# Explicit softmax weights in place of two masked sums in a graph-attention, GRU and mixture-of-experts kernel

## The reference, cut to what matters

```python
h = layernorm(x)
Wh = h @ W;  src = Wh @ a[:256];  dst = Wh @ a[256:]
e = leaky_relu(src + dst.T, 0.2)
att = softmax(where(adj > 0, e, -9e15), axis=1)
gi = (att @ Wh) @ w_ih.T + b_ih
gh = h @ w_hh.T + b_hh
r, z = sigmoid(i_r + h_r), sigmoid(i_z + h_z)
x = x + (1 - z) * tanh(i_n + r * h_n) + z * h
# then: layernorm, gate logits to 16 experts, top 2, expert FFN 256 -> 512 -> 256 with silu, weighted sum, added to x
```

## Time and profile before

| | us |
|---|---|
| median of 3 runs | 1377.35 (1371.5 to 1383.42) |
| the profiled execution, its own time | 1370.29 |
| its span, first to last instruction | 1368.6 |
| outside the span | 1.7 |

### The profile page before, as it was taken

The page is one execution under the profiler, slowest core; times in us unless marked ns, Lnnn a source line. Parts: engine busy times, 40 slices in busy tenths (PEclk is TensorE's granted clock), DMA queues, the critical chain, the costliest instruction groups (busy, mean ns, idle before and its releaser), DMA issues.

```text
span 1368.6 us, 30563 instructions
## 1 busy us (share of the span) xinstructions
PE 1267.8 (93%) x8305; PEld 1101.5 (80%) x8307; DVE 1065.1 (78%) x2513; ACT 671.5 (49%) x1281; POOL 330.8 (24%) x345
## 2 busy tenths in 40 slices
PE   4668999999999999999999999637999999999995
PEld 2447989898998989899898989536888888888884
DVE  3876688787878878787887878597888888887883
ACT  3554444344444534444444444204666666666662
POOL 1011101111111011111101110004655544555554
PEclk9988999999999999999999999857999999999998
DMA  4123334333333333333343432023343455545430
GB/s 135 55 58 48 57 56 67 54 59 67 57 62 57 69 51 60 66 58 63 56 69 50 63 64 36 27 88 94 48 112 78 94 146 126 133 97 133 93 51 8
DMA packets 61970, 98.00 MB, mean 72 GB/s; under 512 B 9856, under 2 KB 36480, under 8 KB 61920
## 3 DMA queue, kind: packets, MB, share of 16 engines
q0 software_dynamic: 33600, 52.49, 25.8%
q1 hardware_dynamic: 27536, 44.14, 10.0%
q10 hardware_dynamic: 784, 0.79, 0.2%
HBM read 213.18 MB, written 18.81 MB: 170 GB/s over the span
## 4 chain that ended last, share of the span: by engine, by line
PE 83%; DMA 6%; DVE 5%; issue 3%; ACT 1%; DVEq 1%; POOL 1%; POOLq 0%; SPq 0%; ACTq 0%
PE bank L1079 37%; PE bank L1187 13%; PE bank L1201 8%; PE bank L1101 8%; PE bank L1013 6%; DMA out<-ysc,cidx 5%; PE pT L1066 4%; PE bank L1104 4%; PE bank L1120 1%; PE bank L1039 1%; ACT V L516 1%; DVE lane_hot L934 1%; POOL rstd L428 1%; DVE slot_hot L938 1%; DMA scr<-in_L_gnn_w_ih 0%
## 5 line engine op out<-in xcount | busy, mean ns | idle before, releaser
L1079 PE MATMUL bank<-V,mask 128*128 128x258 f32 x4096 | 558.4, 289 | 1.7 <-DVE comb L767 1.0
L1079 PEld LDWEIGHTS bank<-V,mask 128*128 128x128 f32 x4096 | 511.4, 190 | 2.1 <-issue 1.1
L533 ACT ACTIVATE mask<-pT 128x512 fp32r<-128x512 bf16 x512 | 277.9, 597 | 195.4 <-PE pT L1066 195.4
L1187 PE MATMUL bank<-wup,xT 128*128 128x512 f32 x948 | 239.0, 401 | 0.9 <-DVE xT L960 0.9
L1187 PEld LDWEIGHTS bank<-wup,xT 128*128 128x128 f32 x948 | 174.1, 190 | 35.0 <-DVE xT L960 1.3
L955 DVE TENSOR_TENSOR wup<-wexp,wup 128x1024 fp32r<-128x1024 f32 x158 | 185.9, 1218 | 2.2 <-ACT wup L488 1.1
L407 POOL DMA_DIRECT2D adjb<-in_adj x128 | 69.4, 542 | 479.3 <-DVE tbuf L750 455.1
L468 POOL DMA_INDIRECT out<-ysc,cidx x79 | 138.3, 1750 | 174.6 <-DMA out<-ysc,cidx 88.8
L488 ACT ACTIVATE wup<-wexp 128x1024 fp32r x158 | 165.7, 1050 | 9.7 <-DMA wexp<-in_L_ffn_w 9.2
L745 DVE CUSTOM_DVE_ANT_0 gbuf<-Dp,adjb 128x1024 bf16<-128x1024 f32 x128 | 156.3, 1221 | 4.0 <-DVE tbuf L750 0.7
L1201 PE MATMUL bank<-wexp,hidT 128*128 x632 | 150.0, 380 | 2.0 <-DVE ysc L993 1.1
(11 more groups left out here) (148 smaller groups left out, 1327.1 us busy)
## 6 DMA issues: line engine op xcount, KB each, us to landing
wexp<-in_L_ffn_w SPq DMA_DIRECT2D x237, 512.0 KB
adjb<-in_adj POOLq DMA_DIRECT2D x128, 256.0 KB, 4.3
token_rows<-xrow SPq DMA_DIRECT2D x32, 130.0 KB, 2.5
adjb<-in_x SPq DMA_DIRECT2D x32, 128.0 KB, 2.1
xin<-in_x SPq DMA_DIRECT2D x32, 128.0 KB, 2.4
out<-xin SPq DMA_DIRECT2D x32, 128.0 KB, 3.3
xg<-token_rows,gidx POOLq DMA_INDIRECT x79, 3.5
out<-ysc,cidx POOLq DMA_INDIRECT x79, 3.8
```

Source lines behind the costliest of these rows:

```text
L533: ins = nc.scalar.activation(mask[:, c % 2, k, :], pT[c % 2][:, 0:MC], ACT.Relu, scale=sign)
L1079: ins = mm(acc[:, 0:VW], mask[:, c % 2, k, b * P:(b + 1) * P], V[:, j, 2 * k + part, :], start=j == 0 and part == 0, stop=j == T - 1 and p ...
L1187: ins = mm(acc[:, 0:HID], xT[:, r % WR, a, k * P:(k + 1) * P], wup[:, r % 2, n, b, k * HID:(k + 1) * HID], start=(k, a, b) == terms[0], st ...
```

## The change

- **Softmax weights are made explicitly.** ACT computes relu(0.8 (src + dst) / 1024) for a whole row of 4096 columns (`logits`, four pieces of 1024), DVE adds adj - 1 to it and takes the maximum (`less_one`, `mask_logits`), and ACT takes exp (`weights`). The missing fifth of the logit that depends on the column alone stands as a factor in V, and the one that depends on the row alone falls out.
- **Three split products.** PE transposes the float32 weights (four transposes a chunk into a whole bank), ACT writes their rounded part (`chunk_hi`), DVE the rest (`chunk_lo`), and PE multiplies hi with V hi, hi with V lo, lo with V hi: 12 matmuls of 258 columns a chunk, into one bank, which alternates from tile to tile. Two chunks are transposed ahead, with three buffers.
- **W is folded.** V holds the scaled normalised x, no longer x @ W. wT's first half becomes W @ w_ih.T, made once in the set-up. The source and target terms come from h @ (W a): two columns (`source_term`) and a broadcast product (`target_terms`).
- **The GRU products stand behind chunks 0 and 1** in PE's order, split in two, and `transpose_x2` stands at the start; `transpose_h` stands behind chunk 3. `rz_tanh` stands at chunk 3 and `copy_hT` and `n_tanh` at chunk 5 in ACT's order.
- **All graph loops are written out**, with constants as semaphore values.
- x is loaded in eight DMAs of 512 KB; POOL makes the rests of V (`value_lo`).

The diff, cut to its core:

```diff
-        V = sb("V", [P, T, 4, VW], F32R, gs)
-        mask = sb("mask", [P, 2, 2, MC], F32R, gs)
+        V = sb("V", [P, T, 2, VW], F32R, gs)
+        E = sb("E", [P, 2, N], F32, gs)
+        pc = sb("pc", [P, 3, 2, MC], F32R, gs)
...
# POOL
+            def value_lo(g):
+                pool.wait_ge(s_hi, g + 1)
+                nc.gpsimd.tensor_tensor(V[:, g * 4:g * 4 + 4, 1, 0:F], xb[:, g % 2, :, :],
+                                        V[:, g * 4:g * 4 + 4, 0, 0:F].bitcast(F32), ALU.subtract).then_inc(s_lo, 1)
...
+                        pool.wait_ge(s_ms, (i + 1) * Q + q + 1)
+                        load_adj(i + 2, q)
...
# ACT
+            def logits(n, q):
...
+                if n >= 2 and q == 0:
+                    act.wait_ge(s_tr, (n - 1) * CPT)
+                nc.scalar.activation(E[:, n % 2, cols], Dp[:, cols], ACT.Relu, bias=sS[:, n:n + 1]).then_inc(s_pre, 1)
+            def weights(n, q):
+                act.wait_ge(s_nmx, n + 1)
+                nc.scalar.activation(E[:, n % 2, cols], E[:, n % 2, cols], ACT.Exp, scale=1.0 / LSC,
+                                     bias=nmu[:, n % 2, 0:1]).then_inc(s_ex, 1)
+            def chunk_hi(C):
+                act.wait_ge(s_tr, C + 1)
+                if C >= 3:
+                    act.wait_ge(s_mm, C - 2)
+                act_copy(pc[:, C % 3, 0, :], pT[C % 3][:, :]).then_inc(s_ph, 1)
...
+            def body(i):
+                if live(i, 3):
+                    act.wait_ge(s_t2, i - 2)
+                    act_copy(xn2T[:, :, :].rearrange("p k m -> p (k m)"), tp[:, 0:F]).then_inc(s_t2e, 1)
+                if i + 1 < T:
+                    for q in range(Q):
+                        logits(i + 1, q)
                 for c in range(CPT):
+                    if live(i, 0):
+                        chunk_hi(i * CPT + c + 2)
+                    if 1 <= c < 1 + Q and i + 1 < T:
+                        weights(i + 1, c - 1)
+                    if c == 3 and live(i, 2):
+                        rz_tanh(i)
+                    if c == 5 and live(i, 1):
+                        copy_hT(i)
+                    if c == 5 and live(i, 2):
+                        n_tanh(i)
+                    if c == 4 and live(i, 3):
+                        gate_exp(i)
...
# DVE
+            def less_one(n, q):
+                dve.wait_ge(s_adj[q], n * 16 + 16)
+                V_.tensor_scalar(adjb[:, q, :], adjb[:, q, :], 1.0, None, ALU.subtract).then_inc(s_am, 1)
+            def mask_logits(n, q):
...
+                V_.tensor_tensor_reduce(out=E[:, n % 2, cols], in0=E[:, n % 2, cols], in1=adjb[:, q, :], scale=1.0,
+                                        scalar=-1e30, op0=ALU.add, op1=ALU.max,
+                                        accum_out=dmx[:, n % 2, q:q + 1]).then_inc(s_ms, 1)
+            def chunk_lo(C):
+                dve.wait_ge(s_ph, C + 1)
+                V_.tensor_tensor(pc[:, C % 3, 1, :], pT[C % 3][:, :], pc[:, C % 3, 0, :].bitcast(F32),
+                                 ALU.subtract).then_inc(s_plo, 1)
...
+            def body(i):
+                ahead = i + 1 < T
+                if ahead:
+                    less_one(i + 1, 0)
+                    less_one(i + 1, 1)
+                if live(i, 1):
+                    combine(i - 1)
+                    remake_xn(i - 1)
+                if ahead:
+                    mask_logits(i + 1, 0)
+                    less_one(i + 1, 2)
+                    mask_logits(i + 1, 1)
+                    less_one(i + 1, 3)
+                    mask_logits(i + 1, 2)
+                for c in range(CPT):
+                    if live(i, 0):
+                        chunk_lo(i * CPT + c + 2)
+                    if c == 0 and ahead:
+                        mask_logits(i + 1, 3)
+                        row_max(i + 1)
+                    if c == 1 and live(i, 3):
+                        route_top(i)
+                    if c == 2 and live(i, 2):
+                        gru_logits(i)
+                    if c == 3 and live(i, 3):
+                        route_weights(i)
+                    if c == 4 and live(i, 2):
+                        gru_n(i)
+                    if c == 6 and live(i, 2):
+                        gru_out(i)
+                    if c == 7 and live(i, 2):
+                        norm2(i)
...
# PE: set-up
+            for t in range(T):
+                transpose_xn(t)
+                if t >= 1:
+                    source_term(t - 1)
+                if t % 4 == 0 and t >= 4:
+                    target_terms(t // 4 - 1)
+                if 5 <= t < 18:
+                    weights_step(t - 5)
...
# PE: graph loop
+                for b in range(JB):
+                    j = c * JB + b
+                    hi, lo = (pc[:, C % 3, k, b * P:(b + 1) * P] for k in range(2))
+                    mm(acc[:, 0:VW], hi, V[:, j, 0, :], start=j == 0, stop=False)
+                    mm(acc[:, 0:VW], hi, V[:, j, 1, :], start=False, stop=False)
+                    ins = mm(acc[:, 0:VW], lo, V[:, j, 0, :], start=False, stop=j == T - 1)
...
+            def transpose_x2(i):
+                pe.wait_ge(s_ln2, i - 2)
...
+            def body(i):
+                if live(i, 3):
+                    transpose_x2(i)
+                if live(i, 3) and not live(i, 0):
+                    gate(i)
                 for c in range(CPT):
+                    if live(i, 0):
+                        transpose_weights(i * CPT + c + 2)
+                        accumulate(i, c)
+                    if c == 0 and live(i, 2):
+                        gru_rz(i)
+                    if c == 1 and live(i, 2):
+                        gru_n(i)
+                    if c == 0 and live(i, 3) and live(i, 0):
                         gate(i)
+                    if c == 3 and live(i, 1):
+                        transpose_h(i)
```

More of the change, by code:

```diff
@@ L522, in _ @@
-            tile_iterations(act, values)
-            for k in range(2):
-                act_copy(V[:, :, 2 * k, F], BD[:, :, k]).then_inc(s_vh, 1)
-            def masks(i, c, st):
-                C = i * CPT + c
-                act.wait_ge(s_tr, C + 1)
-                if st is None or st * CPT + c >= 2:
-                    act.wait_ge(s_mm, C - 1)
-                for k, sign in enumerate((2.0, -2.0)):
-                    ins = nc.scalar.activation(mask[:, c % 2, k, :], pT[c % 2][:, 0:MC], ACT.Relu, scale=sign)
-                ins.then_inc(s_mask, 1)
@@ L539, in rz_tanh, with n_tanh @@
+            for q in range(Q):
+                logits(0, q)
+            value_hi(NG - 1)
+            act_copy(V[:, :, 0, F], bD[:, :]).then_inc(s_vh, 1)
+            for q in range(Q):
+                weights(0, q)
+            chunk_hi(0)
+            chunk_hi(1)
+            def rz_tanh(i):
                 act.wait_ge(s_rz, i - 1)
                 nc.scalar.activation(rz, rz, ACT.Tanh, scale=0.5).then_inc(s_rzt, 1)
-            def n_tanh(i, u):
+            def n_tanh(i):
                 act.wait_ge(s_np, i - 1)
@@ L587, in copy_slot_xT @@
+            for i in range(LAST):
+                body(i)
             def copy_slot_xT(s, r, st):
@@ new lines, in _ @@
+            statistics(0)
+            statistics(1)
+            normalise(0)
+            dve.wait_ge(s_cld[0], 16)
+            dve.wait_ge(s_cld[1], 16)
+            for kb in range(KB):
+                for h in range(2):
+                    link(V_.tensor_tensor_reduce(out=wdump, in0=Wn[:, kb, :], in1=a_row[:, h * F:h * F + F], scale=1.0,
+                                                 scalar=0.0, op0=ALU.mult, op1=ALU.add, accum_out=wa[:, kb, h:h + 1]))
+            V_.tensor_copy(wrep[:, :, :], wa[:, :, 1:2].broadcast_to([P, KB, P])).then_inc(s_wa, 1)
@@ L792, in gru_n, with gru_out @@
                                         op1=ALU.add).then_inc(s_np, 1)
-            def gru_out(i, u, st):
+            def gru_out(i):
+                u = i % 2
                 dve.wait_ge(s_nt, i - 1)
@@ L830, in route_weights @@
                 V_.tensor_tensor(xrow[:, v, F + 1:F + 2], rt[:, 1:2], xrow[:, v, F:F + 1], ALU.mult).then_inc(s_row, 1)
-            piece(0, 0, 0, 0)
-            for k in range(2):
-                dve.wait_ge(s_vh, k + 1)
-                V_.tensor_tensor(V[:, :, 2 * k + 1, F], BD[:, :, k], V[:, :, 2 * k, F].bitcast(F32),
-                                 ALU.subtract).then_inc(s_vd, 1)
+            dve.wait_ge(s_const, CONSTS)
+            less_one(0, 0)
+            less_one(0, 1)
+            mask_logits(0, 0)
@@ L882, in _ @@
+            for i in range(LAST):
+                body(i)
+            dve.wait_ge(s_x1s, T * 16)
             dve.wait_ge(s_rk, 2)
@@ L1070, in accumulate, with transpose_xn @@
-            def accumulate(i, c, st):
-                pe.wait_ge(s_mask, i * CPT + (c + 1))
-                if c == 0 and after(st, 0, 1):
-                    pe.wait_ge(s_af, i)
+            def transpose_xn(t):
+                pe.wait_ge(s_xn, t + 1)
+                if t >= 2:
```

(22 more changed lines are left out.)

733 lines of the change are left out of this document (328 added, 405 removed).

## The result

The changed kernel takes 1402.24 us (median of four runs, 1397.07 to 1403.61), the kernel before on the same chip 1374.77 (1371.5 to 1383.42). The ratio is 1.018, with a 95% interval from 1.013 to 1.024: slower by 1.3 to 2.4%, where 1351 us, faster by 1.4%, was forecast. It lies outside the range too (1315 to 1395). The profiled execution took 1401.48 us, with a span of 1399.7 against 1368.6.

A forecast was written before the change was run, and what follows sets the result against it. PE was taken to bound the loop, waits from engine to engine the set-up. Set-up -35, iterations 0 and 1 -3, iterations 2 to 31 +13, tail +6 sum to -19 on 1370.3: 1351 us, range 1315 to 1395.

The forecast's parts named there:

- the set-up: Stage before the first attention product: that product at 72 us (bounds 64 and 80) against 107.3, so -35 us.
- The 8.5: Set-up, PE: 13 weight steps, 12 x 0.33 us for transposes and 5.2 for the folded product, put at 8.5 in all.
- The bound that I took from the kernel before: Set-up: upper bound of 7.6 us for a group of four tiles, where 5.5 was taken.
- rival 4: Set-up gains little, its chain staying at 7.6 us a group: first product at 90, 1369 us, no change; chance 0.1.
- The loop: Iterations 2 to 31: 24.4 us each for 29 iterations, 22 for iteration 2; +13 us (+2 to +45) on 716.5.
- The ring: Graph loop: waits from norm2 through transpose_x2, PE, ACT's gate_exp and DVE's route_weights back to norm2, 24.4 us an iteration.
- rival 2: Graph loop: PE's clock falls in its 2.5 us wait, 1.8 us more an iteration, +52: 1403 us; chance 0.12.
- that at 102: Set-up before the change: PE's 2.8 us wait at 102.19, followed by half clock; taken as the threshold for the clock falling.
- The tail: Iterations 32 to 34: x2 ahead of the GRU products, rounds of 13.2, 13.5 and 4.2, 31 us against 25: +6.
- iterations 0 and 1: First two graph iterations: 18.2 us each plus 1 for a slow start, against 40.6 before: -3.
- Rival 3: Graph loop: iteration of 25.5 us, 1351 + 32 = 1383 us, slower by 1%; chance 0.16.
- Rival 1: Graph loop: PE's count right, 22 us an iteration, -70: 1285 us; half of it 1316; chance 0.12 in all.

## Why the prediction was wrong, point by point

**The step that failed: the set-up, 72 us forecast and 114.3 measured.** I built it from PE's sum for a group (5.5 us) and set POOL aside with the words that it "has room for over 4 us a group". As an amount of work that is right: a rest takes 2.34 us, as estimated. What counts is where it stands. It waits for ACT's copy, which stands in ACT's order behind three tiles of a later group; those need the power that is queued right ahead of the rest, and the next power is queued behind it. That makes a ring through four engines, of 11.1 us in the group shown, and I never followed it, though for the loop I did exactly that. PE's target terms stand in it too, at 3.2 to 3.8 us rather than the 1.7 of the sum, since the clock is low there. Mending the order gives 23.3 us, taking the rests off POOL 32.8. The first product then comes at 81.5. Of the 9.5 us still missing to the forecast, 3 are the discount from the 75 that the sum gave to the 72 taken, which nothing in it carried; 3.2 are the groups and weight steps (11.7 to 67.4 us, 55.7 rather than 8 x 5.5 + 8.5 = 52.5); 2.1 are the end (14.1 from the last target terms on, not 12); the rest is the start. The 8.5 is itself a slip: 12 x 0.33 + 5.2 is 9.2.

The bound that I took from the kernel before was misread as well. "30.5 us for four groups by the powers of L428" fits no four groups of that trace: 30.50 is the time at which its second power starts. From there the powers start 9.5 to 11.5 us apart (30.50, 40.43, 49.95, 59.67, 69.20, 80.65 and 90.17 us), so a group took 9.9 us, not 7.6. With 9.9 a group, the prediction's own sum for rival 4, a chain that stays as it was, gives a first product at 10.5 + 8 x 9.9 + 8.5 + 12 = 110 us and not at 90.

**The loop, +13 forecast and +15.5 measured.** The ring was found and had the right length: 24.0 us in clean iterations, between the bounds 24.0 and 24.9, 0.4 under the value taken. I kept the middle of the bounds; records in a row overlap fully here. The rest came from rival 2, the clock, which was one of the alternatives and happened in part: 1.6 us in 12 of 28 iterations (priced at 1.8). "It decides from the point where the wait is as long as that at 102" (2.8 us) was too high a bar: 2.5 us were enough, sometimes. The deviations nearly cancel: 28 iterations are 11.2 us shorter by the ring and 18.2 longer by the clock, and the ends of the stage 4.6 shorter, so the term looks better than its parts were. That rival 2's total, 1403, is close to the 1402 measured is luck: it had 52 us from the clock in the loop and nothing from the set-up, where it was 18 and 42.

**Inside the ring, one reading was wrong.** It went through route_weights, and I had put 2.5 us of DVE's rest down to that wait. The wait is there (2.76 us), but without it the iteration is only 0.3 us shorter: the way through PE's own queue to the last chunks is nearly as long. What both share is norm2 ahead of PE's first instruction, and moving that gave 22.12.

**The tail, +6 forecast and +10.9 measured.** The order's cost was right in kind. The clock was left out: behind a wait of 6.7 us the GRU products take 6.18 us rather than 3.59, and that adds 2.6 us in that round. The rounds forecast at 13.2, 13.5 and 4.2 us took 13.9, 17.1 and 4.5; what made the rest of the difference was not looked into.

**What held:** chunks of 12 products and 4 float32 transposes at 1.95 us (1.87 to 1.95 measured), less_one at 0.4 (0.42), iterations 0 and 1 at -3 (-2.3), the experts at 0. The 1024-wide activations with a bias took 1.14 us, not the 1.05 of a plain copy; ACT had room for it. Rival 3 (a ring of 25.5) did not come about as a ring. Rival 4 (the set-up gains little, first product at 90) had the right place and not half the size, at a chance of 0.1, and by the reading above its size was too small from the start. Rival 1's 1285 should read 1281 (1351 - 70).

## What to carry to other kernels

An engine's free time says nothing about a step that waits: in an in-order queue ask what the step waits for, what is queued behind it, and whether the one needs the other in the next round; do this for the set-up with the same care as for the loop. Where a ring of waits is long, look for the second-longest before pricing the removal of one wait, and prefer the edit that all of them share. A bound engine that is given a wait of a couple of microseconds can lose a good part of it again by its clock (here 1.6 us behind waits of 2.5, and 2.8 behind one of 2.3), and even idle filler there can pay.

## What was not expected of the hardware

**The clock falls behind some waits and not behind others of the same length.** In the kernel after, waits of 2.5 us on PE once an iteration left 16 of 28 iterations whole and made 12 long, in six pairs; other runs with the same loop had 9 to 17. With a wait of 2.2 us it was 4 of 28, and with waits of 0.7 to 1.0 us none, also where these were what 14 idle transposes had left of the 2.5. The Trainium skill (TensorE: Matmul & The Clock Gate, What's actually happening, the table of states) has the array fall to the low clock once it has been idle; the runs agree for 6.7 us and for part of the waits of 2.5. What sets which of those it is was not found.

**POOL's long subtraction stops DVE.** Beside a 2.35-us POOL instruction DVE's four normalising instructions took 3.28 to 3.50 us rather than 1.38, and a mask_logits (two inputs) 3.36 rather than 1.21:

```profile
79.03 1.21 DVE L737 CUSTOM_DVE_ANT_0 E<-E,adjb 128x1024 f32<-128x1024 f32 x1
...
80.51 3.36 DVE L737 CUSTOM_DVE_ANT_0 E<-E,adjb 128x1024 f32<-128x1024 f32 x1
```

That is the run with POOL's order changed, where a rest started on POOL at 80.42. The Trainium skill (SBUF — State Buffer, Who interferes with whom) states it: DVE and POOL share a pair of ports that one of them holds for a whole instruction, and the other blocks; DVE needs it for two inputs in SBUF and for its two-port modes. The runs agree. The prediction had weighed POOL's speed beside DVE, and not this rule. In the kernel after no normalising was stretched, since DVE waited for POOL there; two mask_logits were, by 2.9 us together (1.98 and 3.36 us), which would not have changed the sign of the forecast.
